# First stage of a two-layer transformer kernel: rounding by conversion to int32, a Relu as lower clip, and three changes of order

## The reference

```
def fake_quant(x, scale, zp):
    q = clip(round(x / scale + zp), 0, 255)
    return (q - zp) * scale

x = x + fake_quant(layernorm(x)) @ fake_quant(ctx)     # first block, per batch: 256x512 @ 512x512
h = act_qdq(layernorm(x))                              # second block: min and max over all of h,
                                                       # then rounded to 16 bits
x = x + ffn(h, weights rounded to 4 bits in blocks of 32)
x = x + attention(layernorm(x), ctx)                   # K and V are made of ctx alone
x = x + experts(layernorm(x))
```

## Time and profile before

| | us |
|---|---|
| median of 3 runs | 834.78 |
| lowest and highest of them | 833.89, 836.24 |
| the profiled execution | 832.8 |
| its span, first to last instruction | 831.0 |
| busy in the span: TensorE | 721.8 |
| VectorE | 638.7 |
| ScalarE | 515.8 |
| GpSimd | 514.8 |

### The profile page before, as it was taken

The page is one execution under the profiler, slowest core; times in us unless marked ns, Lnnn a source line. Parts: engine busy times, 40 slices in busy tenths (PEclk is TensorE's granted clock), DMA queues, the critical chain, the costliest instruction groups (busy, mean ns, idle before and its releaser), DMA issues.

```text
span 831.0 us, 13580 instructions
## 1 busy us (share of the span) xinstructions
PE 721.8 (87%) x3443; PEld 340.6 (41%) x3443; DVE 638.7 (77%) x1374; ACT 515.8 (62%) x968; POOL 514.8 (62%) x488
## 2 busy tenths in 40 slices
PE   0597989835694996999999999999999688999998
PEld 0243444422331342444444444444444253444443
DVE  6885666979787578788888888888888767666655
ACT  4565655757857427777777777777776634655540
POOL 1995665656667347777888888888884414344330
PEclk9899999978998898999999999999999999999998
DMA  8211213211135315787666666666655512332311
GB/s 320 87 64 38 65 38 102 74 41 51 38 65 116 87 48 155 176 188 176 124 146 143 145 143 145 144 144 147 151 101 102 102 40 76 110 104 90 114 38 50
DMA packets 164500, 89.06 MB, mean 107 GB/s; under 512 B 154082, under 2 KB 154338, under 8 KB 161523
## 3 DMA queue, kind: packets, MB, share of 16 engines
q1 hardware_dynamic: 164466, 88.67, 42.5%
HBM read 49.85 MB, written 1.05 MB: 61 GB/s over the span
## 4 chain that ended last, share of the span: by engine, by line
PE 62%; DVE 14%; POOL 10%; issue 7%; ACT 4%; DMA 2%; SPq 1%; DVEq 0%; POOLq 0%; ACTq 0%
PE ps L937 19%; PE ps L938 19%; PE ps L939 19%; DVE arena L1279 4%; DVE arena L1282 2%; ACT arena L640 2%; POOL arena L469 2%; POOL arena L461 2%; PE ps L1127 1%; DVE arena L1276 1%; DMA arena<-arena 1%; POOL rk L486 1%; POOL arena L490 1%; SPq L368 1%; PE ps L1022 1%
## 5 line engine op out<-in xcount | busy, mean ns | idle before, releaser
L937 PE MATMUL ps<-arena 128*128 128x512 f16 (+2 forms) x996 | 383.6, 385 | 25.4 <-DVE arena L1282 9.7
L938 PE MATMUL ps<-arena 128*128 128x512 f16 (+2 forms) x996 | 383.6, 385 | 0.0
L939 PE MATMUL ps<-arena 128*128 128x512 f16 (+2 forms) x996 | 382.5, 384 | 0.0
L640 ACT ACTIVATE arena<-arena 128x512 f16<-128x512 f32 (+9 forms) x392 | 260.9, 692 | 86.9 <-POOL arena L597 29.6
L1282 DVE SCALAR_TENSOR_TENSOR arena<-ps,arena 128x512 f32<-128x512 f32 (+2 forms) x182 | 123.0, 702 | 51.5 <-ACT arena L640 44.0
L937 PEld LDWEIGHTS ps<-arena 128*128 128x128 f16 (+1 forms) x996 | 99.3, 100 | 146.0 <-issue 35.3
L939 PEld LDWEIGHTS ps<-arena 128*128 128x128 f16 (+1 forms) x996 | 99.3, 100 | 120.8 <-issue 8.3
L938 PEld LDWEIGHTS ps<-arena 128*128 128x128 f16 (+1 forms) x996 | 99.1, 100 | 110.3 <-issue 6.7
L597 POOL TENSOR_SCALAR arena<-arena,rden 128x512 f32<-128x512 f32 x128 | 114.6, 895 | 25.3 <-DVE rden L1625 16.2
L1276 DVE TENSOR_TENSOR arena<-arena 128x512 f16<-128x512 f32 (+2 forms) x146 | 108.4, 777 | 5.3 <-ACT arena L640 4.7
L640 ACT ACTIVATE arena<-ps 128x512 f16<-128x512 f32 (+2 forms) x114 | 63.9, 589 | 77.9 <-PE ps L939 39.5
(11 more groups left out here) (126 smaller groups left out, 696.1 us busy)
## 6 DMA issues: line engine op xcount, KB each, us to landing
arena<-in_moe_w SPq DMA_DIRECT2D x18, 768.0 KB, 4.3
arena<-in_ffn_w SPq DMA_DIRECT2D x33, 256.0 KB, 2.7
arena<-in_wq SPq DMA_DIRECT2D x8, 1024.0 KB, 5.3
arena<-in_wo SPq DMA_DIRECT2D x8, 1024.0 KB, 5.5
arena<-in_kv_w SPq DMA_DIRECT2D x4, 1024.0 KB, 5.3
arena<-arena SPq DMA_TRANSPOSE x144, 3.3
arena<-in_ctx SPq DMA_DIRECT2D x1, 2048.0 KB, 9.0
arena<-in_ctx_t SPq DMA_DIRECT2D x1, 2048.0 KB, 13.4
```

The lines of the kernel that those rows point to most:

```text
L640: return a.activation(out_, in_, ACT.Copy, scale=scale, bias=bias)
L937: pe.matmul(out_, lhs[0], rhs[0], start=first, stop=False)
L938: pe.matmul(out_, lhs[0], rhs[1], start=False, stop=False)
L939: return pe.matmul(out_, lhs[1], rhs[0], start=False, stop=last)
```

## The change

1. The rounding of `xn` and of the scaled context is done by the conversion to int32 on writing. Of `xn` this leaves two full-size instructions (128x2048) where there were three; of the context two where there were four. ScalarE's scaling of the context becomes a `Relu` that writes int32, so it clips at zero too.
2. ScalarE copies the turned `q1` out after the first piece of the context's split, and no longer after the fourth.
3. GpSimd's second power stands ahead of the four `kw_low` of the first quarter.
4. TensorE runs units 0 and 1, `spread(0)`, units 2 to 4, `hidden_transposes(0)`, units 5 to 8. ScalarE's `v_out` and `hidden_high` follow that order.

```
-                a.activation(half, half, ACT.Identity, bias=par[:, 3:4], scale=pc[:, 1:2]).then_inc(ctx_scaled, 1)
+                a.activation(ctx_int[:, b * KD:(b + 1) * KD], half, ACT.Relu, bias=par[:, 3:4],
+                             scale=pc[:, 1:2]).then_inc(ctx_scaled, 1)
...
-            own.link(ts(flat(xn), flat(xn), par[:, 2:3], ALU.add, MAGIC, ALU.add))
-            own.link(ts(flat(xn), flat(xn), MAGIC, ALU.max, MAGIC + 255.0, ALU.min))
-            ts(flat(q1), flat(xn), MAGIC + 128.0, ALU.subtract).then_inc(q1_ready, 1)
+            own.link(ts(flat(xn_int), flat(xn), par[:, 2:3], ALU.add, 0.0, ALU.max))
+            ts(flat(q1), flat(xn_int), 255.0, ALU.min, 128.0, ALU.subtract).then_inc(q1_ready, 1)
             for b in range(B):
-                half = flat(ctx_raw[:, b * KD:(b + 1) * KD])
                 v.wait_ge(ctx_scaled, b + 1)
-                own.mark(ts(half, half, MAGIC, ALU.add, MAGIC, ALU.max))
-            own.wait(own.n)
-            for b in range(B):
-                half = flat(ctx_raw[:, b * KD:(b + 1) * KD])
-                ts(flat(q2[:, b * KD:(b + 1) * KD]), half, MAGIC + 255.0, ALU.min, MAGIC + 128.0, ALU.subtract)\
-                    .then_inc(q2_ready, 1)
+                ts(flat(q2[:, b * KD:(b + 1) * KD]), flat(ctx_int[:, b * KD:(b + 1) * KD]), 255.0, ALU.min, 128.0,
+                   ALU.subtract).then_inc(q2_ready, 1)
...
             pe.wait_ge(ct_lo, KD)
             pe.wait_ge(row_terms, 1)
-            for u in range(4):
+            for u in range(2):
                 v_unit(u)
             spread(0)
-            for u in range(4, MT - 1):
+            for u in range(2, 5):
                 v_unit(u)
             hidden_transposes(0)
-            v_unit(MT - 1)
+            for u in range(5, MT):
+                v_unit(u)
             pe.wait_ge(xt_lo, 1)
             v_unit(MT)
```

More of the change, by code:

```diff
@@ L129, in block_kernel @@
         ctx_raw = carve(150, (MT, D))
+        ctx_int = carve(150, (MT, D), I32)
+        xn_int = carve(8, (NT, D), I32)
         q2 = carve(166, (MT, D), BF16)
@@ L497, in _ @@
                 ct_low(k)
+            rstd(1)
             for k in range(KD):
                 kw_low(0, k)
-            rstd(1)
             divide(0)
@@ L646, in _, with q1_turned @@
                 half = ctx_raw[:, b * KD:(b + 1) * KD]
-                a.activation(half, half, ACT.Identity, bias=par[:, 3:4], scale=pc[:, 1:2]).then_inc(ctx_scaled, 1)
+                a.activation(ctx_int[:, b * KD:(b + 1) * KD], half, ACT.Relu, bias=par[:, 3:4],
+                             scale=pc[:, 1:2]).then_inc(ctx_scaled, 1)
+            def q1_turned():
+                for k in range(KD):
+                    a.wait_ge(q1t_ps, k + 1)
+                    copy(q1t[:, k], bank(k).bitcast(BF16)[:, 0:TOK]).then_inc(q1t_ready, 1)
             a.wait_ge(in_ctt, 16)
@@ L652, in _ @@
                 copy(ct[0][:, k], ctx_t_raw[:, k]).then_inc(ct_hi, 1)
+                if k == 0:
+                    q1_turned()
             def kw_high(c, pieces=range(KD)):
@@ L659, in kw_high @@
                     copy(kw[0][:, c % 2, k * D:(k + 1) * D], kw_raw[:, k]).then_inc(kw_hi, 1)
-            for k in range(KD):
-                a.wait_ge(q1t_ps, k + 1)
-                copy(q1t[:, k], bank(k).bitcast(BF16)[:, 0:TOK]).then_inc(q1t_ready, 1)
             kw_high(0)
@@ L722, in _ @@
             round_weights(2)
-            for u in range(3, MT - 1):
+            v_out(3)
+            v_out(4)
+            hidden_high(0, 1.0)
+            for u in range(5, MT + 1):
                 v_out(u)
-            hidden_high(0, 1.0)
-            v_out(MT - 1)
-            v_out(MT)
             def weight_high(n):
```

## The result

The kernel after takes 840.12 us (median of 19 runs, 835.55 to 844.84), the kernel before on the same chip 834.6 (19 runs, 829.59 to 838.95). The ratio is 1.0071, 95% interval 1.0051 to 1.0091, which is 5.9 us slower (4.3 to 7.6); the two medians themselves lie 5.5 apart. The prediction was 840.3 with a range from 837.0 to 843.3.

A forecast was written before the change was run, and what follows sets the result against it. Two near-equal paths, VectorE's and TensorE's, bound the stretch up to the transposes. Late units and two moved behind the transposes cost +5.2 to +6.2, taken as +5.5: 834.78 + 5.5 = 840.3 us, range 837.0 to 843.3.

The forecast's parts named there:

- the other end: VectorE's rounding: dear price for reading int32, one element per cycle, 2.3 us per instruction against 1.14 taken.
- rival (c): New forms dear: slow Relu or table load delays ScalarE, variance and power by 1 to 3.5 us; 841.5 to 844; 7%.
- Rival (d): Conversions save nothing, int32 read at half speed; hidden behind ScalarE up to 28.8, no other time; part of the forecast.
- nearly 7: GpSimd ahead of the second power: idle from 29.7 to 36.5, waiting for the variance, nearly 7 us.
- buys nothing: GpSimd's second power: was not late before, starting at 38.48 right behind the variance, so moving it gains nothing.
- The upper end: VectorE's four normalising instructions, each meeting a GpSimd kw_low or divide: 1 to 2.7 us added, upper end 2.7.
- the first nine matmuls after the long wait take 0.42 each, at the lower of the two clock levels, before and after alike: TensorE from unit 0: nine matmuls at 0.42 us in both kernels, so units 0 and 1 end at 49.7.
- what I gave (59.5 to 60.8, at most 1 us late): Transposes behind the exchange: where they were, 0 to 1 us late, at 59.5 to 60.8.
- where I had taken 5.5: Delay at the weight loop's start: +5.2 us with transposes on time, +6.2 with them 1 us late, +5.5 taken.
- Rival (b): Part of the delay absorbed later, in the loop over the feed-forward weights: 836 to 837; 9%.

The follow-up runs named there:

- e6: Kernel before with only the int32 conversions and the Relu, q1 still copied after the whole context split: 835.49 us, ratio 1.0010.
- e3: Changed kernel with the power and the units' order both put back, leaving conversions, Relu and early q1 copies: 831.60 us, ratio 0.9972.
- e4: Kernel before with only the second power moved ahead of the four kw_low: 840.32 us, ratio 1.0089.
- e2: Changed kernel with the units back in their old order, the power still ahead of the kw_low: 838.26 us, ratio 1.0044.
- e1: Changed kernel with the second power back behind the four kw_low, the new units' order kept: 838.73 us, ratio 1.0061.
- e5: Kernel before with only the new units' order: 842.54 us, ratio 1.0103.
- e9: e3 with the block scales of the second and third tile moved behind the rounded state: 832.21 us, ratio 0.9983.
- e7: e3 with five units instead of four ahead of the exchange, only unit 8 behind the transposes: 828.75 us, ratio 0.9941.
- e8: e6 with five units instead of four ahead of the exchange: 829.84 us, ratio 0.9942.
- e10: e9 with five units instead of four ahead of the exchange: 831.52 us, ratio 0.9953.

## Why the prediction was right, point by point

**The new forms (edit 1).** Right. Reading int32 costs 1.17 us per instruction, against the 1.14 taken and 2.3 as the other end; writing it is free. `Relu` costs `Identity`'s price, so rival (c) falls. Rival (d) did not come up.

**ScalarE and VectorE (edit 2).** Right within 0.2 us: row terms at 28.92 for 28.8 with no wait, first addition at 29.66 for 29.45, variance at 36.59 for 36.5, normalisation at 40.32 for 40.4. Part of the 0.2 is a profiled execution that starts later altogether (the first rounding at 14.46 for 14.14). What I had not seen is what the copies' old place does to the row sums and the product once edit 1 is in: without edit 2, in e6, the row terms wait for `rsum`, the variance comes 1.05 us later than in e3, and the median is 3.9 us above it.

**The power (edit 3).** Right: waited 6.97 for "nearly 7", unit 0 at 42.63 for 42.6. That the old order would start it 2.9 us earlier than before was right too: 34.31 in e3 is 2.86 earlier. My sentence that moving it "buys nothing" holds for e4, 1.0089.

**The normalisation.** The upper end came, as I took it: four instructions of 4.82 us in sum where they took 2.96.

```profile
40.32 4.82 DVE L1288 TENSOR_SCALAR arena<-arena,mv,rs 128x512 f32<-128x512 f32 x4
...
50.05 0.16 DVE L1398 TENSOR_REDUCE ext<-mm 128x2 f32<-128x8 f32 x1
```

They take 4.82 in e2 and e4 too, which also have the power ahead. In e1, where the `kw_low` are done by then, they take 3.26, and in e5, where GpSimd is idle beside most of them, 1.82. The Trainium skill, page "SBUF — State Buffer", section "Who interferes with whom", has VectorE in its two-port modes and GpSimd lock each other out for whole instructions; the trace agrees, with 3.0 us more for these four beside `kw_low` and `divide` than beside an idle GpSimd.

**The units (edit 4).** The mechanism was right, and one term was mis-sized. The step that failed reads: "the first nine matmuls after the long wait take 0.42 each, at the lower of the two clock levels, before and after alike". It was fourteen, from 42.63 to 48.56. That is five more at 0.21 us, 1.05 us, and units 0 and 1 ended at 50.7 and not 49.7. The extremes were ready at 50.21 (50.05 and 0.16), so TensorE set the exchange, and VectorE did not. The exchange then took 1.68 us (50.72 to 52.40) for 1.26 before: the scaling of `row` took 0.69 us where it had taken 0.27. A small instruction behind it took 0.93 us for 0.45. So the transposes came at 61.18, 1.38 us late and 0.4 past the end of what I gave (59.5 to 60.8, at most 1 us late); unit 8 followed at 72.18, past its 71.9, and the loop started 6.56 us late where I had taken 5.5. The ratio of the runs says 5.9 us and the two medians 5.5, and the interval holds 6.56 as well. That the medians came within 0.2 us of 840.3 is therefore in part luck: the number is fixed to about 1.7 us either way, and the profile's own delay was a microsecond longer than the forecast's.

**Behind the loop's start.** Right: 760.3 us for 759.2 to the end. In e1 to e4, e6 and e9 it is 758.6 to 759.4, in e7 756.9, and in e5, e8 and e10, whose profiled executions had a mean granted clock of 0.950, 0.948 and 0.950, 763.6, 764.8 and 763.2. Most of that lies in one stretch: between the second and the third exchange these three take 54.1, 54.5 and 56.2 us at a granted clock of 0.73, 0.73 and 0.70, and the kernel before, e3 and e7 50.7 or 50.8 at 0.80. Rival (b), part of the delay absorbed later, isn't seen where the delay is.

**What I had only half said.** The prediction adds edit 3 and edit 4 as if both were needed for the 5.5 us: the units start late, and two of them are moved. The runs show that each is enough. With edit 3 alone four late units push the exchange by 5.2 us against e3 (54.33 for 49.15); with edit 4 alone TensorE stands idle ahead of the exchange and pays two units behind the transposes. Put together, edit 4 fills in for edit 3: the late start leaves room for two units only, and two are left. That is why the change as a whole costs hardly more than either half, and why undoing one half looks like a poor remedy.

## What to carry to other kernels

Where two paths meet at a point (here the exchange), count the work that the order lets the waiting engine do ahead of it; a reorder there is right if it fills the wait and wrong if it empties it, and the wait in brackets at that point says by how much. An instruction whose input comes late must not be put at the head of an in-order queue on which others wait, however small it is: its own 1.0 us was never the price, the 7 us in front of it was. And test two edits by undoing them together as well as one by one, since one by one they gave 0.8 and 2.1 us here and together 7.8.

## What the runs showed of the hardware

**How many matmuls run at the lower clock after a wait did not follow from the wait.** Ahead of unit 0 TensorE waited 5.90 us (nine slow matmuls), 5.81 (seven, e5), 8.32 (twelve, e7), 8.76 (nine, e3), 9.33 (fourteen, e1), 8.37 and 8.50 (eleven and ten, e10 and e9), 12.93 (nine, e4), 16.64 (seven, e2) and 16.86 (fourteen, after). The two last have nearly the same wait and the same program on TensorE through units 0 and 1, and differ by seven matmuls, 1.5 us. Slow is a pitch of 0.42, at the 1.2 GHz level (granted clock 0.50 in the kernel before from 37.10 to 41.00), fast 0.216, at 2.4 (1.00 from 41.00 to 49.50). Ahead of the weight loop all of these except e9 and e10, and e6 and e8 too, waited for 2.97 or 2.98 us, and the slow ones behind that were six (before, e2, e6), eight (after, e1, e4, e5), eleven (e8) and none (e3, e7). In e8 the clock fell after a wait of 1.62 us at the exchange, where I had written that it would stay, and eight matmuls behind it were slow; in e3 TensorE waited for 2.50 us at the same place, and none was. e3 and e8 around the loop's start, by the windows (the last three numbers are granted clock, DMA share, GB/s):

```profile
70.00:74.00 4.00, 3.48 (x20) 2.10 (x21) 1.60 (x5) 1.94 (x4) 3.50 (x5) 1.00 0.23 66
```

```profile
68.00:75.00 7.00, 5.93 (x16) 2.74 (x17) 2.59 (x7) 1.74 (x3) 4.70 (x6) 0.51 0.26 75
```

What decides it is open; a forecast has to carry some 1.5 us for each such wait.

**The time of a run goes with the granted clock.** Of the kernel after, 835.55 us came with a mean of 0.955 and 844.84 with 0.945; of e8, 826.79 with 0.962 and 835.67 with 0.948. In each of the eleven kernels timed against the kernel before, 0.01 of mean granted clock goes with 3.8 to 6.6 us. Nine us between runs of one kernel are more than the whole change, so only many runs side by side can tell such edits apart. The mean can't be used to compare kernels that wait differently, since a long wait can itself be at 0.50, as TensorE's from 34.00 to 42.60 is in the kernel after.

**Small instructions of VectorE can be held up as long as large ones of GpSimd last.** The scaling of `rsum`, 128x4, in the kernel after and in e5:

```profile
23.66 2.08 DVE L1288 TENSOR_SCALAR rsum<-rsum,pc 128x4 f32<-128x4 f32 x1
```

```profile
28.43 0.23 DVE L1280 TENSOR_SCALAR rsum<-rsum,pc 128x4 f32<-128x4 f32 x1
```

In the first, GpSimd had begun a low part of 2.1 us at 23.57, and the small instruction ended with it, at 25.74. In the kernel before the same instruction stands ahead of the row terms (1.48 us in its profile, 0.23 in e5, which has the same code there), and moves them: its `rsum` was there at 30.52, and the row terms started at 30.55, where in e5 they start at 29.39. After the change ScalarE is later than it, so even 2.08 us cost nothing. Not every instruction of GpSimd does this: beside the power of 1.02 us from 36.84 on, VectorE's small ones kept their pace in the kernel after:

```profile
37.38 0.17 DVE L1288 TENSOR_SCALAR dsc<-dsc 128x16 f32<-128x16 f32 x1
```
